# One core, a routed feed-forward layer: x fetched from the input for each tile instead of copied into x_rows, and four edits beside it

## The reference, cut to what matters

```python
# _L0_cond_ref: x as 64 quaternions per token, scaled by spectral_gate (one factor per quaternion,
# the same for all frequencies), multiplied from both sides
x_right   = hamilton(x_filtered, q_right_conj)
x_rotated = hamilton(q_left_n, x_right)            # q_left = cond_256, both normalized
# _L0_ffn_ref, on x_rotated
logits = einsum('bsd,de->bse', x, router_w) + router_b
top1 = argmax(softmax(logits), axis=-1)
for i in range(8):
    h = einsum('bsd,df->bsf', x, w1[i]) + b1[i]    # 256 -> 2048
    a, g = split(h, 2, axis=-1)
    y = einsum('bsh,hd->bsd', a * sigmoid(g), w2[i]) + b2[i]   # 1024 -> 256
    out = out + where((top1 == i)[..., None], y, 0.0)
# the kernel's result
x + _L0_ffn_ref(_L0_cond_ref(x, ...), ...)
```

## Time and profile before

| what | value |
|---|---|
| median of three runs | 208.42 us |
| profiled execution | 207.35 us, its span 205.6 us |
| TensorE busy | 191.6 us (93%) |
| VectorE busy | 146.1 us (71%) |
| ACT busy | 125.1 us (61%) |
| POOL busy | 87.7 us (43%) |
| moved by DMA | 42.34 MB, mean 206 GB/s |

### The profile page before, as it was taken

How to read it: one execution, slowest core, us unless ns; L and a number is a source line. 1 busy time by engine, 2 the same in 40 slices (tenths; PEclk the granted TensorE clock), 3 DMA queues, 4 the chain that set the end, 5 groups by cost and what they waited for, 6 DMA issues and landing times.

```text
span 205.6 us, 4304 instructions
## 1 busy us (share of the span) xinstructions
PE 191.6 (93%) x1451; PEld 181.2 (88%) x1453; DVE 146.1 (71%) x296; ACT 125.1 (61%) x222; POOL 87.7 (43%) x138
## 2 busy tenths in 40 slices
PE   7997867999999999999999999999999999999960
PEld 3777733999999999999999999999999999999950
DVE  4928944678854888398869869995999488839510
ACT  2454770385756676486875958695777667648310
POOL 8002544631700645445467084555637364004403
PEclk9999999999999999999999999999999999999997
DMA  4999925879948161787198469618861976001001
GB/s 136 383 402 385 311 64 190 261 260 328 308 128 357 51 213 47 249 333 238 34 390 302 154 199 406 232 38 303 344 205 53 336 277 208 0 0 37 28 5 43
DMA packets 20054, 42.34 MB, mean 206 GB/s; under 512 B 2472, under 2 KB 14905, under 8 KB 17978
## 3 DMA queue, kind: packets, MB, share of 16 engines
q1 hardware_dynamic: 15808, 31.54, 42.8%
q0 software_dynamic: 4000, 10.50, 16.1%
q10 hardware_dynamic: 218, 0.01, 0.1%
HBM read 35.74 MB, written 8.13 MB: 213 GB/s over the span
## 4 chain that ended last, share of the span: by engine, by line
PE 90%; DMA 4%; issue 1%; DVE 1%; POOL 1%; ACT 1%; DVEq 0%; POOLq 0%
PE y_ps L1208 8%; PE g_ps L1176 8%; PE g_ps L1169 8%; PE a_ps L1169 8%; PE y_ps L1210 8%; PE a_ps L1176 8%; PE y_ps L1209 8%; PE a_ps L1172 8%; PE g_ps L1172 8%; PE y_ps L1120 3%; PE y_ps L942 3%; DMA x_turn<-x_rows,g_idx 2%; PE a_ps L1018 2%; PE a_ps L1099 2%; DMA x_rows<-arena 2%
## 5 line engine op out<-in xcount | busy, mean ns | idle before, releaser
L854 DVE SCALAR_TENSOR_TENSOR arena<-a_ps,b_t,arena 128x336 f32<-128x336 f32 (+1 forms) x64 | 33.3, 521 | 27.7 <-PE a_ps L1176 24.1
L579 ACT ACTIVATE arena<-g_ps,b_t 128x336 f32<-128x336 f32 (+1 forms) x64 | 32.2, 503 | 32.4 <-PE g_ps L1176 32.2
L452 POOL DMA_INDIRECT out_dram<-x_turn,s_idx x22 | 28.5, 1295 | 47.3 <-DVE x_turn L874 35.4
L740 DVE TENSOR_TENSOR w_lo<-w_raw,w_hi 128x1024 fp32r<-128x1024 f32 x32 | 37.7, 1221 | 9.1 <-DMA x_turn<-x_rows,g_idx 5.2
L438 POOL DMA_INDIRECT x_turn<-x_rows,g_idx x24 | 30.6, 1275 | 31.1 <-DMA out_dram<-x_turn,s_idx 17.3
L1208 PE MATMUL y_ps<-u_hi,w_hi 128*128 128x336 f32 (+2 forms) x128 | 38.1, 298 | 0.3 <-issue 0.3
L1210 PE MATMUL y_ps<-u_lo,w_hi 128*128 128x336 f32 (+2 forms) x128 | 37.5, 293 | 0.0
L1209 PE MATMUL y_ps<-u_hi,w_lo 128*128 128x336 f32 (+2 forms) x128 | 37.5, 293 | 0.0
L1169 PE MATMUL g_ps<-xr_hi,w_hi 128*128 128x336 f32 (+2 forms) x128 | 36.1, 299 | 0.0
L1169 PE MATMUL a_ps<-xr_hi,w_hi 128*128 128x336 f32 (+2 forms) x128 | 35.6, 294 | 0.0
L1172 PE MATMUL a_ps<-xr_hi,w_lo 128*128 128x336 f32 (+2 forms) x128 | 35.5, 293 | 0.0
(11 more groups left out here) (181 smaller groups left out, 306.8 us busy)
## 6 DMA issues: line engine op xcount, KB each, us to landing
w_raw<-in_L_ffn_w_dram SPq DMA_DIRECT2D x16, 1024.0 KB, 7.9
w_raw<-in_L_ffn_w_dram SPq DMA_DIRECT2D x16, 512.0 KB, 4.6
x_own<-in_x_dram SPq DMA_DIRECT2D x4, 512.0 KB, 6.0
x_rows<-x_own SPq DMA_DIRECT2D x4, 512.0 KB, 11.1
x_rows<-arena SPq DMA_DIRECT2D x8, 256.0 KB, 3.4
x_turn<-x_rows,g_idx POOLq DMA_INDIRECT x24, 6.0
out_dram<-x_turn,s_idx POOLq DMA_INDIRECT x22, 3.7
x_own<-x_rows,g_idx POOLq DMA_INDIRECT x8, 5.6
```

The source lines that it names most:

```text
L579: nc.scalar.activation(sig[:, c % SIG_RING, 0:n], pair[c % RING][1][:, 0:n], ACT.Sigmoid, bias=b1_t[:, bass.ds(e * (2 * NC) + (NC + c), 1) ...
L740: V.tensor_tensor(unit_of(w1_lo, u), raw_unit(u), unit_of(w1_hi[:, :].bitcast(F32), u), ALU.subtract)\
L854: V.scalar_tensor_tensor(u32[:, c % (8 - SIG_RING), 0:n], pair[c % RING][0][:, 0:n], b1_t[:, bass.ds(e * (2 * NC) + c, 1)], sig[:, c % SIG ...
```

## The change

It does five things. (1) x_rows has rows of 1 KB, the rotated x alone; the four copies of x are gone, and gather(i) issues, behind its four gathers from x_rows, four more from the input x with the same indices, into the second half of each row of the buffer. They count on a semaphore of their own, x_fetched, for which the next gather and the additions wait. (2) The sizes of all tiles stand in one packed word, which VectorE writes before the rest of ctrl and TensorE reads alone; size codes are stored as 4 minus the step, so that code 0 ends the loop. q_spare is computed behind the first indices. (3) One visit of far code is left, at the very start, and its landing stands behind leaf 1; the five warming matmuls behind it go, and wr's product moves from behind group 4 to behind group 6 of the transposes. (4) The rotations of pairs 2 and 3 stand ahead of the ranks. (5) The end goes by block: ACT biases the second half of the last tile in two pieces, 128 columns first, TensorE turns the first half and then the second block by block into PSUM tensors of their own, and VectorE adds the first half at once and the second by block.

```diff
-    x_rows = nc.dram_tensor("x_rows", (TOK, 2 * DIM), F32, kind="Internal").ap()
+    x_rows = nc.dram_tensor("x_rows", (TOK, DIM), F32, kind="Internal").ap()
 # SP
-            for g in range(4):
-                sp.wait_ge(x_loaded[g], 16)
-                sp.dma_start(x_rows_v[:, 4 * g:4 * g + 4, DIM:ROW], x_tok[:, 4 * g:4 * g + 4, :]).then_inc(x_part_written, 16)
...
-                sp.dma_start(x_rows_v[:, 2 * b:2 * b + 2, 0:DIM], x_rot[:, 2 * b:2 * b + 2, :]).then_inc(x_rows_written, 16)
+                sp.dma_start(x_rows_v[:, 2 * b:2 * b + 2, :], x_rot[:, 2 * b:2 * b + 2, :]).then_inc(x_rows_written, 16)
 # POOL
-                        out=pairs[buffer_of(i)][:, s * ROW:(s + 1) * ROW], out_offset=None, in_=x_rows,
+                        out=pairs[buffer_of(i)][:, s * ROW:s * ROW + DIM], out_offset=None, in_=x_rows,
...
+                for s in range(NSUB):
+                    nc.gpsimd.indirect_dma_start(
+                        out=pairs[buffer_of(i)][:, s * ROW + DIM:(s + 1) * ROW], out_offset=None, in_=x_flat,
+                        in_offset=bass.IndirectOffsetOnAxis(ap=g_idx[:, i * NSUB + s:i * NSUB + s + 1], axis=0),
+                        bounds_check=row_bound, oob_is_err=False).then_inc(x_fetched, 16)
...
-            pool.wait_ge(x_part_written, 4 * 16)
...
                 if i + 1 < NE:
+                    pool.wait_ge(x_fetched, (i + 1) * NSUB * 16)
                     if i + 1 >= YB:
                         wait_scattered(i + 1 - YB)
                     gather(i + 1)
 # ACT, last tile
-                    for h in range(KH):
-                        biased(i, e, h, 0, FIRST, yt_done[h])
+                    biased(i, e, 0, 0, min(n, FIRST), yt_done[0])
+                    biased(i, e, 1, 0, P, yt_first)
+                    biased(i, e, 1, P, min(n, FIRST), yt_done[1])
 # VectorE
+            V.tensor_scalar(packed[:, :], left, float(len(SIZES) * sum(PLACES)), None, ALU.add).then_inc(packed_ready, 1)
+            dve.wait_ge(moved_ready, 1)
+            link(V.scalar_tensor_tensor(q_spare[:, :], past[:, :], float(NSUB) / BIG, moved[:, :], ALU.mult, ALU.mult))
+            link(V.tensor_tensor(q_spare[:, :], q_spare[:, :], q_at[:, :], ALU.add))
...
+            def add_by_block(i, blocks, done):
+                dve.wait_ge(x_fetched, (i + 1) * NSUB * 16)
+                rows = rows_of(i)
+                dve.wait_ge(half_turned, i - NE + 2)
+                V.tensor_tensor(rows[:, 0:blocks, 0], y_half[0][:, 0:blocks * P].rearrange("p (s d) -> p s d", d=P),
+                                rows[:, 0:blocks, 0], ALU.add)
+                for s in range(blocks):
+                    dve.wait_ge(block_turned, (i - NE + 1) * NSUB + s + 1)
+                    last = V.tensor_tensor(rows[:, s, 1], apart[s][:, 0:P], rows[:, s, 1], ALU.add)
+                    if done is not None:
+                        last.then_inc(done, 1)
+                return last
...
-            for s in range(2):
-                dve.wait_ge(gathered[s], 16)
+            dve.wait_ge(gathered[0], 16)
 # TensorE
             visit(1)
             pe.wait_ge(still_set, 1)
-            keep_warm(early_ps, 5)
...
-                if f == 3:
-                    visit(2)
-                if f == 4:
+                if f == 6:
                     pe.wait_ge(wr_loaded, 16)
...
-            rotate_blocks(1)
+            for b in range(1, GROUPS):
+                rotate_blocks(b)
             pe.wait_ge(consts_ready, CONSTS)
             pe.wait_ge(in_row_ready, 1)
...
-            for b in range(2, NB // 2):
+            for b in range(GROUPS, NB // 2):
                 rotate_blocks(b)
-                if b == 5:
-                    visit(4)
...
-            pe.wait_ge(ctrl_ready, 1)
-            last_tile = load_last(pe)
-            visit(6)
-            keep_warm_long(late_ps, 2)
+            pe.wait_ge(packed_ready, 1)
...
                     leaf(low)
                     here = nc.cur_bb
                     pe.br("top")
+                    if low == 1:
+                        landing_behind(1)
...
-            turn_back_rows(NSUB)
+            pe.wait_ge(yt_done[0], at1)
+            for s in range(NSUB):
+                last = T.transpose(y_half[0][:, s * P:(s + 1) * P], yt[:, s * P:(s + 1) * P], ident[:, :])
+            last.then_inc(half_turned, 1)
+            for s in range(NSUB):
+                if s < 2:
+                    pe.wait_ge((yt_first, yt_done[1])[s], at1)
+                T.transpose(apart[s][:, 0:P], yt[:, ITEM + s * P:ITEM + (s + 1) * P], ident[:, :]).then_inc(block_turned, 1)
+            pe.wait_ge(ctrl_ready, 1)
+            last_tile = load_last(pe)
             with pe.If(last_tile < tile):
-                here = nc.cur_bb
-                pe.br("done")
-                nc.switch_bb("behind_done", parent=here)
+                jump("done", "behind_done")
```

More of the change, by code:

```diff
@@ L55, in adaln_moe_ffn_kernel @@
     LEFT = 3
-    SPECIAL = len(SIZES)
+    PLACES = [1 << (LEFT * e) for e in range(NE)]
     EPS = 1e-8
@@ L105, in adaln_moe_ffn_kernel @@
         s_idx = sb("s_idx", TAB * NSUB, I32)
-        ctrl = sb("ctrl", 3 + TAB, I32)
+        ctrl = sb("ctrl", 2 + TAB, I32)
+        packed = sb("packed", 1, I32)
+        places = sb("places", NE)
         ident = sb("ident", P)
@@ L556, in _ @@
                 act.sem_inc(yt_done[h], 1)
+            act.sem_inc(yt_first, NE)
             act.sem_inc(sig_done[NC - 2], 1)
@@ L799, in _ @@
                 slot_one_hot(n)
-            dve.wait_ge(moved_ready, 1)
-            link(V.scalar_tensor_tensor(q_spare[:, :], past[:, :], float(NSUB) / BIG, moved[:, :], ALU.mult, ALU.mult))
-            link(V.tensor_tensor(q_spare[:, :], q_spare[:, :], q_at[:, :], ALU.add))
             def indices(idx_ps, at, count):
@@ L833, in _ @@
             V.tensor_scalar(ctrl[:, 1 + NE:1 + TAB], owner, float(MORE), None, ALU.add)
-            V.memset(ctrl[:, 1 + TAB:2 + TAB], 0)
-            link(V.tensor_tensor(places[:, :], places[:, :], steps, ALU.mult))
-            link(V.tensor_reduce(left, places[:, :], AX.X, ALU.add))
-            V.tensor_scalar(ctrl[:, 2 + TAB:3 + TAB], left, float(SPECIAL << (LEFT * (NE - 1))), None, ALU.add)\
-                .then_inc(ctrl_ready, 1)
+            V.memset(ctrl[:, 1 + TAB:2 + TAB], 0).then_inc(ctrl_ready, 1)
             dve.wait_ge(idx_spare_summed, 1)
@@ L955, in visit @@
                 nc.switch_bb(f"back{line}", parent=visited_from[line])
-            def landing(line):
-                here = nc.cur_bb
-                pe.br(f"past{line}")
-                nc.switch_bb(f"landing{line}", parent=visited_from[line])
-                pe.nop()
-                pe.br(f"back{line}")
-                nc.switch_bb(f"past{line}", parent=here)
             visit(1)
             pe.wait_ge(still_set, 1)
-            keep_warm(early_ps, 5)
             pe.wait_ge(consts_ready, 1)
@@ L1044, in _ @@
                 .then_inc(b1_turned, 1)
-            landing(1)
             pe.wait_ge(b1_t_done, 1)
@@ L1053, in _ @@
             last.then_inc(idx_summed, 1)
-            visit(5)
             pe.wait_ge(still32_set, 1)
@@ L1233, in leaf, with jump, by_size @@
                 second_half(size, 1)
-            def by_size(size, low, high):
-                if low == high:
-                    if low == SPECIAL - 1:
-                        with pe.If(size >= SPECIAL):
-                            here = nc.cur_bb
-                            pe.br("special")
-                            nc.switch_bb("behind_special", parent=here)
+            def jump(to, behind):
+                here = nc.cur_bb
+                pe.br(to)
+                nc.switch_bb(behind, parent=here)
+            def by_size(code, low, high):
+                if low == high:
                     leaf(low)
@@ L1248, in by_size @@
                 middle = (low + high + 1) // 2
-                with pe.If(size < middle):
-                    by_size(size, low, middle - 1)
+                with pe.If(code > len(SIZES) - middle):
+                    by_size(code, low, middle - 1)
                 with pe.Else():
-                    by_size(size, middle, high)
+                    if middle == high == len(SIZES) - 1:
+                        with pe.If(code < 1):
+                            jump("special", "behind_special")
+                    by_size(code, middle, high)
             begin = nc.cur_bb
```

70 lines of the change are left out of this document (30 added, 40 removed).

## The result

The changed kernel took 219.81 us at the median of four runs (217.12 to 221.31), the kernel before 208.71 on the same chip. The ratio, with two disturbed runs of the changed kernel left out, is 1.043 (95% interval 1.032 to 1.054): slower. The profiled execution took 218.75 us, its span 216.9.

A forecast was written before the change was run, and what follows sets the result against it. The prediction took TensorE to bound the middle, where gathers were in time by only 1.7 us. Head -1.2, tail -1.35 and middle +0.3 gave -2.25: 206.2 us on the median's scale, range 204.5 to 212.5.

The forecast's parts named there:

- the other five visits ... at nothing: Head: dropping five far-code visits costs nothing, covered by the first tile's wait for rows; uncovered, 0.18 to 0.38 us each.
- a case that got 9 in 100: Rival, head lost: early visit and later clock cancel the gain, or unvisited leaves miss; 207.5 to 212 us, chance 0.09.
- The sum by three misses (+10.2): Leaves no longer visited: by the skill's rule they miss on first use, three times 3.41 us, +10.2 us.
- The walk through POOL's issues: Middle: issues followed one by one; gather(5) 1.7 us late, gather(6) 4.8, no TensorE wait at tiles 2 to 7.
- One slot missed on POOL: Rival, middle: scatter(3) meets the W1 load, gather(6) 9.6 us late, TensorE waits 3.7; 209.9 us, chance 0.30.
- A middle taken between 1.7 and 9.6: Middle: gather(6) 5.7 us late, between cheap and dear issue prices, inside the 6.0 us it could bear.
- the prediction's own loop: Rival, POOL bound: twelve issues at 1.6 plus 4.65 make 23.9 us against 20.2 per tile; 211.2 to 215, chance 0.16.
- Forecast -1.2: Head: early rotations -1.5, early visit and warming +0.6, 1 KB rows -0.3; range -2.5 to +0.7 us.
- the index table, forecast at 26.1: Head: g_idx ready at about 26.1 us with ranks 0.25 later, letting the first gather start at about 27.0.
- up to 0.95: Head: if the early visit costs 3.41 us, up to 0.95 us is lost in the chain to the logits.
- -1.5 from the early rotations: Head: rotations of pairs 2 and 3 ahead of the ranks let the first gather start 1.5 us earlier.
- Forecast -1.35: Tail: the end by block shortens ACT's start to the first scatter from 2.59 to 1.25 us; range 0.9 to 1.7.

The follow-up runs named there:

- the kernel with one wait more: The kernel before, with TensorE waiting for the first W2 half to land before the first leaf: 214.51 us, 1.023.
- part 1 stands alone: The kernel before with only x fetched by four more indirect DMAs and rows of 1 KB: 219.68 us; fetching three subtiles instead of four: 207.38 us.

## Why the prediction was wrong

**The step that failed first** is the one that cost "the other five visits ... at nothing: the first tile waits for its rows, which land last". That cover hides a branch of 0.3 us, not one of 4.2: the leaf's code is needed after the rows, not beside them. The row for it was there, and I priced with it a case that got 9 in 100, for the reason that "the code of the head runs straight into the first leaves", which no row showed. It measured +7.1: 3.3 of stop, 1.3 of a second stop that the profile puts down to no wait either, and the rest, 2.5, is about what the lower clock cost in the kernel with one wait more (2.3). The rule of the Trainium skill, "Runtime: NRT & Kernel Launch", "Instruction fetch mechanics", that a taken branch to code outside the fetched window waits for its fetch, agrees with the far visits and the slow jumps here, 3.3 to 5.0 us each. The sum by three misses (+10.2) had the sign right, the number of misses not: one jump was slow.

**The walk through POOL's issues** ("gather(6) 4.8 late: no wait") was wrong by little, and this was enough: the last scatter came 1.24 us behind the W1 load, less than one issue. The rival "One slot missed on POOL" describes what the traces show: the scatter issued into the W1 load, and gather(6) landing at 160.5, which is 153.4 without the 7.1 us by which tile 5 came later (the rival had about 153.6). Its wait of 3.7 us came as 3.33 and 1.40; the lower clock behind it, it did not have. One issue of 1.3 us more or less decides over 12 us when part 1 stands alone (219.68 against 207.38). A middle taken between 1.7 and 9.6, just inside a room of 6.0, was no ground to call it the likelier case: at the mean price of an issue the prediction's own loop was longer than a tile (23.9 against 20.2 us).

**No term priced the clock behind a stop.** Each stop of TensorE was counted as its own length. The stop by itself cost 4.0 + 2.3 us; the second loss of +6.6 is 4.7 of stop and 1.9 beyond it, most of it the half clock, as far as these numbers show.

**Head.** Forecast -1.2, found 0.0 up to the turn of tile 0. The term that failed is the index table, forecast at 26.1: it stood at 27.34. The early visit itself came as priced (TensorE back at 4.68, the small product of q 0.93 us later than in the earlier trace rows, of "up to 0.95"), but the forecast of the table left it out. Another 0.5 us came between that product and the logits, where TensorE now waited 0.45 us for a load of x; why, no run separates. The ranks started at 19.66, 1.7 us later, not 0.25. The cover "the first tile waits for its rows" failed here as well: with q_spare behind the first indices TensorE stood still 2.23 us, and the turn waited for TensorE.

Part 1 alone won 1.23 us at the first product, as much as was forecast for the whole head. That is luck: the sum had -1.5 from the early rotations, which by themselves won nothing (209.08), and only -0.3 from the rows of 1 KB; it gave the sooner landing of the last write at most 0.3, and it came 0.7 us sooner.

**Tail.** Forecast -1.35, measured -2.4 in the profile and 2.6 us (0.987) by itself. The path to the first scatter was right (1.2 of gain), the sooner landing was not foreseen.

The sum: -1.2 - 1.35 + 0.3 forecast, 0.0 - 2.4 + 7.1 + 0.1 + 6.6 = +11.3 found. The range reached 212.5 because it held one loss at a time; that two rivals could both be true had no place in it.

## What to carry to other kernels

Edits costed at nothing need a row for the cover and for the price without it: here a branch of 3.4 us, seen once at the end of the old profile, was the nearest price, and the jump cost 4.23. Where a serial loop of one engine is nearly as long as the stage that it feeds, count issues at their mean price and ask what transfer the last of them runs into; work that nobody needs yet belongs into the loop's waits, not ahead of them. And a stop of TensorE in a running stage can cost more than its length: here one of 4.0 us cost 6.3.

## What the runs showed of the hardware

With two late visits of far code the jump to the second use of a leaf took 5.03 us; in the changed kernel, with one early visit, it took 0.23. Which of the visits did it, no run separates. An indirect DMA issued about 1 us behind a 2 MB load released POOL 6 us after its issue ended, one issued 4 us ahead of it after 1.9. A stop of 4.01 us at TensorE was followed by about 5.5 us at 1.2 GHz (granted 0.50 from 41.1 to 46.0 us, 1.00 from 47.0). The same lower level came in the head of several kernels with no more than 1 us of idle time just ahead of it, and with the same head in one profile and not in another; no run gave the cause. An issue on POOL that began at 154.34, while VectorE subtracted from 154.30 to 156.58, took 3.16 us instead of 1.00.
